# Edge lists loaded in rows of 2000 bytes, the key arithmetic on GpSimd, part of x issued later: a change to the prologue of a graph and mixture-of-experts kernel

## The chip, the cores and the metric

One core of one Trainium2 chip runs the whole program. The metric is the device time of that core in microseconds (us); lower is better. The kernel before takes 423.84 us, the median of three runs that span 423.71 to 424.52 us.

## What is computed

`x` is 1250 nodes by 512 features, with 40000 edges in two integer lists. `src` holds the node that receives and `dst` the node that is read; `dst` is sorted. The reference, cut to what matters:

```python
def gnn(x, edge_index, W1, b1, W2, b2):          # W1 512x256, W2 256x512
    h = relu(x @ W1 + b1) @ W2 + b2
    row, col = edge_index[0], edge_index[1]       # src, dst
    return h + segment_sum(h[col], row, num_segments=1250)

def ffn(x, W_gate, b_gate, W_thr, b_thr, W_exp, b_exp):   # 8 experts of 512x512
    adapted = softmax(x @ W_gate + b_gate) - sigmoid(x @ W_thr + b_thr) * 0.25
    w = adapted * (adapted >= 0);  w = w / sum(w)  (1 where the sum is 0)
    return sum over e of w[:, e] * (x @ W_exp[e] + b_exp[e])

x = x + gnn(layernorm(x), stack([src, dst]), ...)
x = x + ffn(layernorm(x), ...)
```

## The kernel before, in words

The aggregation is done as matrix products. For each window of 25 read nodes the kernel counts, on TensorE, how many edges lead from each of those nodes to each of the 1250 receiving nodes. That count matrix, moved by DMA into another layout (`a_t`), multiplies the hidden rows `r_sb`. There are 50 windows (NW), five to each of ten tiles of 125 nodes.

The counting compares keys. The receiving node is written as `src = 250*hi + lo` with hi from 0 to 4. One key is `lo`, the other is `pos = 5*dst + hi`. The 40000 edges are cut into 320 chunks (CH) of 125 consecutive edges. A column of `keys` holds a chunk, one edge on each of 125 partitions. For a window, VectorE compares the keys of its chunks with tables of positions (`places`), which gives matrices of zeros and ones in f16 (`hot`, line L552 in `compare`), and TensorE multiplies them (L788 in `count`). ScalarE takes the counts out of PSUM (L390) and SyncE's queue moves them (L282). How many chunks a window has depends on the data, so the loops of `compare` and `count` read their start and length from a table `wtab`.

All this needs a prologue, and the change is in the prologue alone. The order of each engine is written out by hand, one block of code per engine, and engines wait for one another by semaphores:

- **SyncE** (L264, L265) issues the loads of `dst_i` and `src_i`, 80 partitions (ROWS) by 4 (GJ) by 125 edges (EP), then five loads of `x_sb`, then W1 and b1.
- **GpSimd** (L311 on) fills constants: `ident`, `ones`, rows of window bounds, `c_up` and `c_down` (chunk numbers), the step table, then the five tables that ScalarE waits for (`lo_ready` 5, L342), then `zeros`, `self_pos` and `self_lo` (`self_ready` 3, L344 to L351), for which TensorE waits before its zero matmuls.
- **ScalarE** (L354 on) issues the load of partitions 112 to 124 of x (L356, semaphore `x_rest`), makes `places` for windows 0 and 1, copies the transposed keys out of PSUM into `keys` (L374, L377, semaphore `keys_placed`), and goes on with `places` for windows 2 to 4.
- **VectorE** (L448 on) reduces each chunk of `dst_i` to its least and greatest node (L455, L456), finds the chunks that meet each window (L459 to L468, semaphore `hits_ready`), computes the keys (L471 to L477, `keys_ready`), and then derives the table: L480 reads the transposed hits, L483 to L497 give three columns `wcols`, and L500 to L503 write `wtab`. It loads the table's first word, waits for `keys_placed` and begins `compare(0)`.
- **TensorE** (L709 on) waits for `hits_ready` and transposes the hits (L716), waits for `keys_ready` 1 and transposes `lo_f`, waits for 2 and transposes `pos_f` (L722), waits for `wcols_ready` 3 and turns the columns into rows (L727), waits for `self_ready` 3 and clears five banks with zero matmuls (L732), then waits for `wtab_ready` 2 and `keys_placed` 2, raises `hot_used` and starts `count(0)`.

Everything on TensorE is in this order, so a wait for keys holds back the rows of the table too. VectorE's first compare waits for `hot_used`, which TensorE raises only behind its zero matmuls:

```python
pe.wait_ge(self_ready, 3)
for k in range(5):
    z = nc.tensor.matmul(ps_g[:, k * BANK:(k + 1) * BANK], zeros[0:1, 0:128], zeros[0:1, :], ...)
z.then_inc(g_done, 1)
pe.wait_ge(wtab_ready, 2)
pe.wait_ge(keys_placed, 2)
for p in range(4):
    pe.sem_inc(hot_used[p], 1)
```

Behind the prologue come the counting and the hidden layer (to about 165 us), the second matrix product and the second layer norm (to about 210 us), and the expert loop to the end.

## Time and profile before

| | us |
|---|---|
| median of 3 runs (lowest, highest) | 423.84 (423.71, 424.52) |
| the profiled execution's own time | 425.66 |
| its span, first to last instruction | 423.8 |
| TensorE busy (share of the span) | 393.7 (93%) |
| VectorE busy | 294.4 (69%) |
| ScalarE busy | 95.8 (23%) |
| GpSimd busy | 5.1 (1%) |
| mean granted TensorE clock | 0.98 |

The profiled execution took 425.66 us, of which 423.8 us are its span and the rest lies around it. TensorE is PE in the rows (PEld its weight loads), VectorE is DVE, ScalarE ACT, GpSimd POOL, and SyncE's queue SPq. A matmul record's end is modelled, so records of one engine can overlap a little. In a timeline row the first number is the start, the second the length covered, then engine, line, operation, output and inputs, shape, and in brackets the idle time before it. A row with xN merges N records.

### The profile page before, as it was taken

Reading aid. Unit: us, or ns where it says so; the run is one execution under the profiler, and the core shown is the slowest. Engines: PE = TensorE matmul, PEld = TensorE weight load, DVE = VectorE, ACT = ScalarE, POOL = GpSimd, SP = SyncE. Lnnn points to the kernel's source line nnn. Section 1 sums busy time; section 2 is a strip of 40 time slices with the busy share of each in tenths; the row PEclk is TensorE's granted clock in tenths of the full one; section 3 lists DMA queues with packets and bytes.
Section 4 is the critical chain, followed back from the end, with each engine's and each line's share of the span. In section 5 each row is a group of like instructions: output and inputs, shape, how many; then the busy total and the mean of one; then the engine's idle time right before and its main releaser. Section 6 shows DMA issues by size and latency. Waiting matters only on the chain.

```text
span 423.8 us, 6033 instructions
## 1 busy us (share of the span) xinstructions
PE 393.7 (93%) x1964; PEld 246.0 (58%) x1964; DVE 294.4 (69%) x445; ACT 95.8 (23%) x166; POOL 5.1 (1%) x27
## 2 busy tenths in 40 slices
PE   0945999999998999979899999999999999999996
PEld 0422676666654555636566666666666666666663
DVE  3799997954656885299739767575665756657654
ACT  4621243443356551033330100101010010100000
POOL 4000000000000000000000000000000000000000
PEclk9988899999999999899899999999999999999999
DMA  8500013214133222063000203020030300000133
GB/s 179 142 13 12 25 38 108 43 34 139 37 116 111 66 68 71 0 168 127 2 0 2 99 0 101 0 95 5 0 99 0 99 0 0 0 0 0 50 97 97
DMA packets 16680, 23.75 MB, mean 56 GB/s; under 512 B 2792, under 2 KB 9555, under 8 KB 16532
## 3 DMA queue, kind: packets, MB, share of 16 engines
q1 hardware_dynamic: 16254, 22.93, 18.5%
q10 hardware_dynamic: 403, 0.53, 0.6%
q8 instruction: 12, 0.20, 0.2%
q14 instruction: 11, 0.09, 0.1%
HBM read 14.65 MB, written 2.56 MB: 41 GB/s over the span
## 4 chain that ended last, share of the span: by engine, by line
PE 81%; DVE 10%; issue 3%; DMA 2%; DVEq 2%; ACT 0%; ACTq 0%
PE ps_g L860 16%; PE ps_g L862 16%; PE ps_g L861 16%; PE ps_g L766 10%; PE ps_w L788 8%; PE ps_a L754 5%; DVE split L552 3%; DVE x_sb L595 2%; PE ps_a L755 1%; DVE stats L511 1%; DMA dst_i<-in_dst_dram 1%; PE ps_a L745 1%; PE ps_w L781 1%; PE ps_w L793 1%; DVE x_sb L603 1%
## 5 line engine op out<-in xcount | busy, mean ns | idle before, releaser
L861 PE MATMUL ps_g<-we_lo,split 128*125 128x512 f16 x320 | 122.0, 381 | 0.0
L862 PE MATMUL ps_g<-we_hi,split 128*125 128x512 f16 x320 | 122.0, 381 | 0.0
L860 PE MATMUL ps_g<-we_hi,split 128*125 128x512 f16 x320 | 122.0, 381 | 0.0
L552 DVE TENSOR_TENSOR split<-places,keys 125x1536 f16<-125x1536 int16 (+2 forms) x125 | 94.2, 816 | 7.2 <-PE ps_w L788 4.1
L671 DVE SCALAR_TENSOR_TENSOR x_sb<-ps_g,weight_s,x_sb 125x512 f32<-125x512 f32 x80 | 59.9, 749 | 56.3 <-PE ps_g L862 56.2
L788 PE MATMUL ps_w<-split 125*128 125x250 f16 x416 | 60.9, 289 | 11.6 <-DVE split L552 11.6
L676 DVE SCALAR_TENSOR_TENSOR x_sb<-late,weight,x_sb 125x512 f32<-125x512 f32 x80 | 59.9, 750 | 9.5 <-DVE x_sb L671 5.3
L788 PEld LDWEIGHTS ps_w<-split 125*128 125x128 f16 x416 | 40.0, 102 | 34.3 <-DVE split L552 21.5
L860 PEld LDWEIGHTS ps_g<-we_hi,split 128*125 128x125 f16 x320 | 43.9, 137 | 25.9 <-issue 0.6
L862 PEld LDWEIGHTS ps_g<-we_hi,split 128*125 128x125 f16 x320 | 43.9, 137 | 25.6 <-issue 0.4
L861 PEld LDWEIGHTS ps_g<-we_lo,split 128*125 128x125 f16 x320 | 43.9, 137 | 25.5 <-issue 0.6
L766 PE MATMUL ps_g<-late,r_sb 125*128 125x512 f32 (+3 forms) x120 | 54.3, 557 | 0.2
L427 ACT ACTIVATE we_hi<-stage 128x2048 f16<-128x2048 f32 x6 | 11.5, 1911 | 139.4 <-PE ps_g L862 139.4
L365 ACT ACTIVATE places<-iota_pos,win_base 125x512 int16<-125x512 int16 x50 | 35.6, 713 | 0.0
L390 ACT ACTIVATE counts<-ps_w 128x250 f32<-128x250 f32 x50 | 19.0, 380 | 72.0 <-PE ps_w L793 72.0
L568 DVE TENSOR_TENSOR late<-late 125x1250 f32<-125x1250 f32 x8 | 11.7, 1460 | 26.2 <-DMA late<-counts 26.2
L766 PEld LDWEIGHTS ps_g<-late,r_sb 125*128 125x128 f32 x120 | 19.7, 192 | 10.2 <-issue 9.3
L754 PE MATMUL ps_a<-w_sb,xn_t 128*125 128x256 f32 x80 | 19.9, 392 | 0.0
L584 DVE SCALAR_TENSOR_TENSOR we_lo<-stage,we_hi 128x2048 f16<-128x2048 f32 x8 | 18.3, 2285 | 0.0
L754 PEld LDWEIGHTS ps_a<-w_sb,xn_t 128*125 128x125 f32 x80 | 14.2, 187 | 1.8
L781 PE MATMUL ps_w<-self_lo,self_pos 128*128 128x250 f16 x50 | 13.8, 275 | 0.0
L828 PE MATMUL ps_w<-w_sb,early 128*125 128x512 f32 x24 | 11.2, 597 | 0.5 <-ACT early L412 0.5
(125 smaller groups left out, 201.1 us busy)
## 6 DMA issues: line engine op xcount, KB each, us to landing
stage<-in_L_ffn_W_exp_dram SPq DMA_DIRECT2D x8, 1024.0 KB, 5.2
late<-counts SPq DMA_DIRECT2D x50, 122.1 KB
x_sb<-in_x_dram SPq DMA_DIRECT2D x5, 448.0 KB, 9.6
out_dram<-x_sb SPq DMA_DIRECT2D x10, 224.0 KB
late<-in_L_ffn_b_exp_dram SPq DMA_DIRECT2D x1, 2000.0 KB
w_sb<-in_L_gnn_W_dram SPq DMA_DIRECT2D x2, 512.0 KB, 8.5
x_sb<-in_x_dram ACTq DMA_DIRECT2D x1, 260.0 KB
out_dram<-x_sb ACTq DMA_DIRECT2D x10, 26.0 KB
```

What stands on the lines that cost most here:

```text
L365: nc.scalar.activation(places[w % WPT][:, :, 0:SEG], iota_pos[:, :, :], ACT.Identity, bias=win_base[:, w:w + 1], scale=1.0).then_inc(pos_r ...
L390: nc.scalar.activation(counts[q][:, :], ps_w[w % 2][:, 0:LO], ACT.Copy).then_inc(win_out, 1)
L552: nc.vector.tensor_tensor(hot[hot_at(w, p)][:, 0:n, :].rearrange("p c (k x j) -> p (c k) x j", k=SEGS, j=2), places[w % WPT][:, 0:n, :].re ...
L584: nc.vector.scalar_tensor_tensor(out=we_lo[par][:, :], in0=stage[par][:, :], scalar=WSCALE, in1=we_hi[par][:, :], op0=ALU.mult, op1=ALU.su ...
L671: nc.vector.scalar_tensor_tensor(out=x_sb[:, i, :], in0=ps_exp[(TILES * par + i) % RING], scalar=weight_s[:, ds(e, 1), i], in1=x_sb[:, i, ...
L676: nc.vector.scalar_tensor_tensor(out=x_sb[:, i, :], in0=be_sb[:, ds(e, 1), :], scalar=weight[:, i, ds(e, 1)], in1=x_sb[:, i, :], op0=ALU.m ...
L754: nc.tensor.matmul(ps_a[0:R, 0:C], xn_t[:, k, :], w1_sb[:, k, :], start=(k == 0), stop=False)
L766: g = nc.tensor.matmul(ps_g[:, a:z], r_sb[:, i, c * 128:(c + 1) * 128], a_t[i % 3][:, a - c * SW:z - c * SW], start=False, stop=False, ski ...
L788: mm = nc.tensor.matmul(bank[:, 0:LO], hot[hot_at(w, p)][:, c, 0:SEG], hot[hot_at(w, p)][:, c, SEG:SEG + LO], start=False, stop=False, ski ...
L860: nc.tensor.matmul(bank, xhi[:, k, tokens[i]], hi_w, start=(k == 0), stop=False)
L861: nc.tensor.matmul(bank, xhi[:, k, tokens[i]], lo_w, start=False, stop=False)
L862: mm = nc.tensor.matmul(bank, xlo[:, k, tokens[i]], hi_w, start=False, stop=(k == KD - 1))
```

## The change

Five edits belong together.

1. `dst_i` and `src_i` are loaded so that a partition holds 500 consecutive edges, one row of 2000 bytes, and no longer four rows of 500 bytes. A partition's four chunks are now neighbours in number, so `c_up` and `c_down` count by fours.
2. The four key operations on VectorE are taken out. GpSimd computes the keys in seven instructions (of them six calculate and one is the copy of `src_i` to f32). They stand behind the tables for ScalarE and ahead of `zeros`, `self_pos` and `self_lo`. They wait for `src_in`, and among themselves for `hi_step`.
3. `pos` is finished first, `lo` second, and TensorE's transposes and ScalarE's two copies follow in that order.
4. A transpose writes every fourth column of its PSUM bank, and no longer 80 neighbouring ones, so that chunks stand in order in `keys`.
5. The load of the last 13 partitions of x moves on ScalarE's queue from the first place to behind `places` of windows 0 and 1.

The diff, without the renumbered waits of VectorE on `prep`:

```diff
-        hi_a, hi_f, lo_f, pos_f = (early[0:ROWS, k * EP * GJ:(k + 1) * EP * GJ].rearrange("p (j e) -> p j e", j=GJ)
-                                   for k in range(4))
+        hi_a, hi_f, lo_f, pos_f, dst_5 = (early[0:ROWS, k * EP * GJ:(k + 1) * EP * GJ].rearrange("p (j e) -> p j e", j=GJ)
+                                          for k in range(5))
+        src_f = sb("src_f", [ROWS, GJ, EP])[:, :, :]
...
-            sp.dma_start(dst_i[:, :, :], dst.rearrange("(j g e) -> g j e", j=GJ, e=EP)).then_inc(dst_in, 16)
-            sp.dma_start(src_i[:, :, :], src.rearrange("(j g e) -> g j e", j=GJ, e=EP)).then_inc(src_in, 16)
+            sp.dma_start(dst_i[:, :, :], dst.rearrange("(g j e) -> g j e", j=GJ, e=EP)).then_inc(dst_in, 16)
+            sp.dma_start(src_i[:, :, :], src.rearrange("(g j e) -> g j e", j=GJ, e=EP)).then_inc(src_in, 16)
...
-            nc.gpsimd.iota(c_up[:, :], pattern=[[ROWS, GJ]], base=1, channel_multiplier=1,
+            nc.gpsimd.iota(c_up[:, :], pattern=[[1, GJ]], base=1, channel_multiplier=GJ,
...
-            nc.gpsimd.iota(c_down[:, :], pattern=[[-ROWS, GJ]], base=CH, channel_multiplier=-1,
+            nc.gpsimd.iota(c_down[:, :], pattern=[[-1, GJ]], base=CH, channel_multiplier=-GJ,
...
+            pool.wait_ge(src_in, 16)
+            nc.gpsimd.tensor_scalar(hi_a, src_i[:, :, :], 1.0 / LO, -(LO - 1) / (2.0 * LO), ALU.mult, ALU.add).then_inc(hi_step, 1)
+            nc.gpsimd.tensor_copy(src_f, src_i[:, :, :]).then_inc(hi_step, 1)
+            nc.gpsimd.tensor_scalar(dst_5, dst_i[:, :, :], float(HI), None, ALU.mult).then_inc(hi_step, 1)
+            pool.wait_ge(hi_step, 3)
+            nc.gpsimd.tensor_scalar(hi_f, hi_a, ROUND, ROUND, ALU.add, ALU.subtract).then_inc(hi_step, 1)
+            pool.wait_ge(hi_step, 4)
+            nc.gpsimd.tensor_tensor(pos_f, dst_5, hi_f, ALU.add).then_inc(keys_ready, 1)
+            nc.gpsimd.tensor_scalar(hi_a, hi_f, -float(LO), None, ALU.mult).then_inc(hi_step, 1)
+            pool.wait_ge(hi_step, 5)
+            nc.gpsimd.tensor_tensor(lo_f, hi_a, src_f, ALU.add).then_inc(keys_ready, 1)
+
             nc.gpsimd.memset(zeros[:, :], 0.0).then_inc(self_ready, 1)
...
-            act.dma_start(x_sb[112:R, :, :], x.rearrange("(t p) d -> p t d", p=R)[112:R, :, :]).then_inc(x_rest, 16)
             act.wait_ge(lo_ready, 5)
...
+            act.dma_start(x_sb[112:R, :, :], x.rearrange("(t p) d -> p t d", p=R)[112:R, :, :]).then_inc(x_rest, 16)
             key_view = keys[:, 0:CH * REC].rearrange("p (c t) -> p c t", t=REC)
             act.wait_ge(keys_turned, 1)
-            nc.scalar.activation(key_view[:, :, 2:REC], ps_w[0][0:EP, 0:CH].unsqueeze(2).broadcast_to([EP, CH, REC - 2]),
+            nc.scalar.activation(key_view[:, :, 0:2], ps_w[1][0:EP, 0:CH].unsqueeze(2).broadcast_to([EP, CH, 2]),
                                  ACT.Copy).then_inc(keys_placed, 1)
             act.wait_ge(keys_turned, 2)
-            nc.scalar.activation(key_view[:, :, 0:2], ps_w[1][0:EP, 0:CH].unsqueeze(2).broadcast_to([EP, CH, 2]),
+            nc.scalar.activation(key_view[:, :, 2:REC], ps_w[0][0:EP, 0:CH].unsqueeze(2).broadcast_to([EP, CH, REC - 2]),
                                  ACT.Copy).then_inc(keys_placed, 1)
...
-            dve.wait_ge(src_in, 16)
-            nc.vector.tensor_scalar(hi_a, src_i[:, :, :], 1.0 / LO, -(LO - 1) / (2.0 * LO), ALU.mult, ALU.add).then_inc(prep, 1)
-            dve.wait_ge(prep, 6)
-            nc.vector.tensor_scalar(hi_f, hi_a, ROUND, ROUND, ALU.add, ALU.subtract).then_inc(prep, 1)
-            dve.wait_ge(prep, 7)
-            nc.vector.scalar_tensor_tensor(out=lo_f, in0=hi_f, scalar=-float(LO), in1=src_i[:, :, :],
-                                           op0=ALU.mult, op1=ALU.add).then_inc(keys_ready, 1)
-            nc.vector.scalar_tensor_tensor(out=pos_f, in0=dst_i[:, :, :], scalar=float(HI), in1=hi_f,
-                                           op0=ALU.mult, op1=ALU.add).then_inc(keys_ready, 1)
...
-            for a, (key, bank) in enumerate(((lo_f, ps_w[0]), (pos_f, ps_w[1]))):
+            for a, (key, bank) in enumerate(((pos_f, ps_w[1]), (lo_f, ps_w[0]))):
                 pe.wait_ge(keys_ready, a + 1)
                 for j in range(GJ):
-                    turned = nc.tensor.transpose(bank[0:EP, j * ROWS:(j + 1) * ROWS], key[:, j, :],
+                    turned = nc.tensor.transpose(bank[0:EP, 0:CH].rearrange("p (g j) -> p j g", j=GJ)[:, j, :], key[:, j, :],
                                                  ident[0:ROWS, 0:ROWS])
```

The order on GpSimd from the last table for ScalarE on, before (`early` is the buffer that holds `hi_a`, `hi_f`, `lo_f`, `pos_f` and now `dst_5`):

```order
L342 MEMSET keys 125x90
L344 MEMSET zeros 1x512
L345 MEMSET self_pos 128x132
L346 MEMSET self_lo 128x475
L349 AFFINE_SELECT self_pos<-self_pos 25x132 [waits self_base]
L351 AFFINE_SELECT self_lo<-self_lo 25x475
```

And on GpSimd now:

```order
L343 MEMSET keys 125x90
L346 TENSOR_SCALAR early<-src_i 80x500 [waits src_in]
L347 CAST src_f<-src_i 80x500
L348 TENSOR_SCALAR early<-dst_i 80x500
L350 TENSOR_SCALAR early<-early 80x500 [waits hi_step]
L352 TENSOR_TENSOR early<-early 80x500 [waits hi_step]
L353 TENSOR_SCALAR early<-early 80x500
L355 TENSOR_TENSOR early<-early,src_f 80x500 [waits hi_step]
L357 MEMSET zeros 1x512
L358 MEMSET self_pos 128x132
L359 MEMSET self_lo 128x475
L362 AFFINE_SELECT self_pos<-self_pos 25x132 [waits self_base]
```

Seven instructions stand between the tables and `zeros`; what TensorE's zero matmuls wait for comes behind them.

TensorE's prologue now, whose rows are the same as before but for line numbers and the PSUM banks of the keys (`ps_w1` holds `pos`, `ps_w0` holds `lo`):

```order
L720 MATMUL ps_g<-ident,hit_idx 50x80 [waits hits_ready,const_ready]
L720 MATMUL ps_g<-ident,hit_idx 50x80 x7
L726 MATMUL ps_w1<-ident,early 125x80 [waits keys_ready]
L726 MATMUL ps_w1<-ident,early 125x80 x3
L726 MATMUL ps_w0<-ident,early 125x80 [waits keys_ready]
L726 MATMUL ps_w0<-ident,early 125x80 x3
L731 MATMUL ps_a<-ident,wcols 1x50 [waits wcols_ready]
L731 MATMUL ps_a<-ident,wcols 1x50 x2
L736 MATMUL ps_g<-zeros 128x512 [waits self_ready]
L736 MATMUL ps_g<-zeros 128x512 x4
L785 MATMUL ps_w0<-self_lo,self_pos 128x250 [waits wtab_ready,keys_placed]
```

The waits on `keys_ready` at L726 are now for GpSimd, and they stand ahead of the table's rows at L731.

## Rows read from the trace of the kernel before

**Rows 1.** Busy time by stage: length, then each engine, PEclk, DMA share, GB/s
```profile
core 0: us, PE busy (x) PEld busy (x) DVE busy (x) ACT busy (x) POOL busy (x), PEclk, DMA share, GB/s
16.00:50.00 34.00, 23.51 (x129) 12.43 (x128) 33.23 (x53) 8.60 (x16) 0.00 (x0) 0.85 0.05 14
50.00:165.00 115.00, 113.69 (x624) 72.54 (x624) 83.57 (x115) 52.36 (x108) 0.00 (x0) 1.00 0.26 75
...
210.00:424.00 214.00, 210.20 (x979) 132.55 (x978) 137.64 (x185) 15.51 (x11) 0.00 (x0) 0.99 0.12 37
```

**Rows 2.** Timeline of the prologue, 0 to 17 us: DVE, PE, ACT and queues
```profile
0.74 0.37 SPq L264 DMA_DIRECT2D dst_i<-in_dst_dram  x1
0.74 0.65 ACTq L356 DMA_DIRECT2D x_sb<-in_x_dram  x1
...
6.40 0.67 DVE L455 TENSOR_REDUCE cmin<-dst_i 80x4 f32<-80x500 int32 x1 [2.94 <-DMA dst_i<-in_dst_dram]
6.91 0.70 ACT L365 ACTIVATE places<-iota_pos,win_base 125x512 int16<-125x512 int16 x1
...
9.11 0.35 DVE L468 TENSOR_TENSOR hit_idx<-hit,c_down 80x200 f32<-80x200 f32 x1
...
9.61 1.24 PE L716 MATMUL ps_g<-ident,hit_idx 80*50 80x80 f32 x8 [9.61 <-DVE hit_idx L468]
...
10.28 0.67 DVE L475 SCALAR_TENSOR_TENSOR early<-early,src_i 80x500 f32<-80x500 f32 x1
...
11.01 1.97 PE L722 MATMUL ps_w<-ident,early 80*125 80x80 f32 x8 [0.16 <-DVE early L475]
11.47 0.81 DVE L480 TENSOR_REDUCE wmax<-ps_g 50x2 f32<-50x640 f32 x1
12.18 1.24 ACT L374 ACTIVATE keys<-ps_w 125x1280 int16<-125x1280 f32 x1 [4.56 <-PE ps_w L722]
...
13.35 0.15 DVE L497 TENSOR_TENSOR wcols<-wcols,step_col 50x1 f32<-50x1 f32 x1
...
13.55 0.66 PE L727 MATMUL ps_a<-ident,wcols 50*1 50x50 f32 x6 [0.57 <-DVE wcols L497]
...
14.14 2.31 PE L732 MATMUL ps_g<-zeros 1*128 1x512 f16 x5
...
16.07 10.51 DVE L552 TENSOR_TENSOR split<-places,keys 125x1536 f16<-125x1536 int16 x12 [1.40 <-ACT places L365]
```

**Rows 3.** Chain that ended last, in order of time: start, us, what
```profile
0.74 5.63 DMA dst_i<-in_dst_dram
...
26.59 2.98 DVE stats L511 x5
```

**Rows 4.** DMA queue of SyncE: packets, MB, share of 16 engines; 1.5 to 2, 4.5 to 6 us
```profile
q1 hardware_dynamic: 45, 0.02, 33.8%
...
q1 hardware_dynamic: 351, 0.26, 115.3%
```

**Rows 5.** DMA issues: size and us from issue to landing
```profile
src_i<-in_src_dram SPq DMA_DIRECT2D x1, 156.2 KB, 5.9
```

**Rows 6.** DMA packets of all queues, 6 to 7.5 us, then 7 to 16 us
```profile
DMA packets 180, 0.36 MB, mean 239 GB/s; under 512 B 5, under 2 KB 5, under 8 KB 180
...
DMA packets 1450, 2.36 MB, mean 262 GB/s; under 512 B 80, under 2 KB 519, under 8 KB 1450
```

**Rows 7.** Timeline of POOL in the prologue
```profile
2.07 1.15 POOL L331 TENSOR_SCALAR_AFFINE_SELECT step_col<-step_col 50x1 f32<-50x1 f32 x4
3.49 0.56 POOL L337 IOTA iota_pos<- 125x500 int16 x1
...
4.19 0.17 POOL L342 MEMSET keys<- 125x90 int16 x1
4.30 0.52 POOL L344 MEMSET zeros<- 1x512 f16 x1
...
5.80 0.58 POOL L351 TENSOR_SCALAR_AFFINE_SELECT self_lo<-self_lo 25x475 f16<-25x475 f16 x1
```

More of the change, by code:

```diff
@@ L198, in gnn_moe @@
         lo_ready, self_base, self_ready = sem("lo_ready"), sem("self_base"), sem("self_ready")
-        keys_placed = sem("keys_placed")
+        keys_placed, hi_step = sem("keys_placed"), sem("hi_step")
         prep, keys_ready = sem("prep"), sem("keys_ready")
@@ L481, in _ @@
                                     AX_X, ALU.max).then_inc(prep, 1)
-            dve.wait_ge(prep, 8)
+            dve.wait_ge(prep, 6)
             nc.vector.tensor_scalar(wtmp[:, :], wmax[:, 1:2], 1.0, -1.0, ALU.max, ALU.mult).then_inc(prep, 1)
-            dve.wait_ge(prep, 9)
+            dve.wait_ge(prep, 7)
             nc.vector.tensor_scalar(wfirst[:, :], wtmp[:, :], float(CH), None, ALU.add).then_inc(prep, 1)
             nc.vector.tensor_scalar(wcols[:, 0:1], wtmp[:, :], float(CH), float(REC), ALU.add, ALU.mult).then_inc(wcols_ready, 1)
-            dve.wait_ge(prep, 10)
+            dve.wait_ge(prep, 8)
             nc.vector.scalar_tensor_tensor(out=wcount[:, :], in0=wmax[:, 0:1], scalar=wfirst[:, :], in1=ones[0:NW, 0:1],
                                            op0=ALU.subtract, op1=ALU.max).then_inc(prep, 1)
-            dve.wait_ge(prep, 11)
+            dve.wait_ge(prep, 9)
             dve.wait_ge(step_ready, 2)
@@ L493, in _ @@
                                            op0=ALU.add, op1=ALU.mult).then_inc(prep, 1)
-            dve.wait_ge(prep, 12)
+            dve.wait_ge(prep, 10)
             nc.vector.tensor_scalar(wcols[:, 1:2], wsteps[:, :], ROUND, ROUND, ALU.add, ALU.subtract).then_inc(wcols_ready, 1)
@@ L501, in _ @@
             nc.vector.tensor_copy(wtab[:, NW:2 * NW], ps_a[0:1, NW:2 * NW]).then_inc(wtab_ready, 1)
-            dve.wait_ge(prep, 13)
+            dve.wait_ge(prep, 11)
             nc.vector.scalar_tensor_tensor(out=wtab[:, 0:NW], in0=ps_a[0:1, 2 * NW:3 * NW], scalar=float(REC * WORD),
```

## The prediction, made blind

> **What bounds the kernel now.** I read the stages first, then the timeline and the chain of the prologue, then the DMA queues and GpSimd. By stage [rows 1], TensorE is busy 113.69 of 115 us from 50 to 165 us and 210.20 of 214 us from 210 us on; from 16 to 50 us VectorE is (33.23 of 34 us), since it makes the `hot` matrices. Before 16 us neither is near full, and nothing behind the prologue is touched by the diff. So the question is by how much the first compare moves, which starts at 16.07 us [rows 2]. All that follows hangs on it: the same instructions with the same waits, so I expect the rest to shift as a block.
>
> The chain in order of time [rows 3] starts with 5.63 us of waiting for `dst_i`. VectorE's reductions begin at 6.40, its last hits end at 9.46, TensorE transposes them until 10.85, but the reduction of the transposed hits starts only at 11.47, because the key operations stand ahead of it. The table's columns are done at 13.50, its rows start on TensorE at 13.55, the zero matmuls at 14.14, and the compare is 2.52 us behind the rows' start and 1.93 us behind the zeros' [rows 2]. The keys are in place at 12.18 + 1.24 + about 0.6 = 14.0 us and nobody waits for them.
>
> **Loads.** 80 partitions by 4 rows make 320 packets of 500 bytes for each list, and the new form makes 80 of 2000 bytes. The first small packets run shortly before 2 us, the last before 6 us [rows 4]: from 6 to 7.5 us only 5 packets under 512 bytes are left [rows 6]. `src_i` lands at 1.17 + 5.9 = 7.1 us [rows 5], some 1.1 us behind its last packet. Packets of 2 KB go at 262 GB/s [rows 6]. 0.32 MB for both lists then take 1.2 us, half of it for `dst_i`, and the load of `x_rest`, which ran between them on ScalarE's queue, is gone from there. 1.8 + 0.6 + 1.1 = 3.5 us for `dst_i`, 4.1 us for `src_i`; I add 0.3 us to each for the loads of x that now begin earlier, so 3.8 and 4.4. Ends: 3.5 (VectorE's two step operations end there anyway), and 6.37, no gain at all, if a load's time were mostly fixed. I take the value near the lower end because the small packets fill the queue for over 4 us. **VectorE's first reduction moves from 6.40 to 3.9, 2.5 us earlier.**
>
> **VectorE and TensorE up to the table.** The hits end at 9.46 - 2.5 = 6.96, their transposes at 8.35. With the four key operations gone, the reduction follows at 8.4 instead of 11.47, and the columns are done at about 10.4 instead of 13.50. Alone, this path would bring the compare to 10.45 + 2.52 = 12.97 us, a gain of 3.1 us. It isn't alone: TensorE passes the keys first.
>
> **GpSimd.** It ends the tables for ScalarE at 4.36 [rows 7], so it starts on the keys at about 4.45, when `src_i` has landed. No row shows it doing such arithmetic. The nearest: a select over 475 elements takes 0.58 us, an iota over 500 takes 0.56 us. I take 0.585 us for each of the five operations with one input. For the two with two tensor inputs the lower end is 0.585 and I take the double, 1.17, each input being read in its turn. The four selects on `step_col`, each waiting for the one before, take 1.15 us though they are 0.14 to 0.18 us long: a wait on itself costs about 0.15 us, and there are three. Sum: 5 x 0.585 + 2 x 1.17 + 3 x 0.15 = 5.7 us, so `lo_f` is done at 10.17 us. Two paths go on from there:
> - Transposes of `lo`: a group of four took from 10.95 to 12.18, 1.23 us [rows 2]. The rows of the table start at 11.40, later than the columns (10.4), and the compare would follow at 11.40 + 2.52 = 13.92 us.
> - The memsets and selects for `self_ready`, which took from 4.30 to 6.38, hidden until now, come behind `lo_f`: 10.17 + 2.08 = 12.25. The zero matmuls start there instead of at 14.14, and the compare at 12.25 + 1.93 = **14.18 us**. This path is the later one.
>
> GPSIMD Engine Reference of the Trainium skill, section 3.1, gives about 2.6 cycles for an element of a two-input add against one for a one-input body, at 1.2 GHz; that is an estimate of 1.08 us for 500 elements, and the sum would come out 0.2 us lower. No row here shows it.
>
> ScalarE has its `pos` copy (0.71 us, the shorter one) done before `lo` is transposed, then 1.24 us for `lo`: keys in place at 11.40 + 1.24 = 12.65 us, hidden behind the zeros. Were the zeros quick, this would be next. The load of `x_rest` is issued at 7.61 + 0.65 = 8.3 us, while ScalarE idles; even at the 9.6 us that the median load of x took it lands by 18 us, and the layer norm's statistics want it at 26.59 [rows 3] less the shift. Cost nothing; that cover is 6 us wide.
>
> **Collision of GpSimd and VectorE.** Before, GpSimd was finished at 6.38 and VectorE began at 6.40, so no row shows the two side by side. Now VectorE's five operations on hits (0.35 us each, two tensor inputs) run at 5.2 to 7.0 us beside GpSimd's first ones. Ends: nothing, and strict turns (rival 1, 2.1 us later). I take one VectorE operation, 0.4 us, since most of GpSimd's chain lies behind 7 us.
>
> **Sum.** 16.07 - 14.18 = 1.9 us less, plus 0.4 = 1.5 us less. On the profiled execution (425.66 us, of which the span is 423.8) that is 424.2; the median stands 1.8 us below that execution, so the forecast is **422.3 us**. A measurement can tell from no change about 0.2% here, 0.85 us.
>
> **Rival 1: the two engines take turns.** SBUF — State Buffer of the Trainium skill, section "Who interferes with whom", says that a VectorE instruction with two SBUF inputs contends with a GpSimd instruction that reads SBUF, and the later one is blocked for the whole instruction; the trace before can't show it. As a mechanism of this kernel: each of the five hit operations waits for a GpSimd operation in flight (0.585, once 1.17) and GpSimd for it (0.35). Alternating from 5.2 us on, the hits end at about 10.3, `lo_f` at 11.5. TensorE then ends hits at 11.7, `pos` at 12.8, `lo` at 13.8; the compare comes at 13.8 + 2.5 = 16.3 us. The loads' gain is eaten: 424.0 us, within 0.5 us of no change. For it: the overlap is sure. Against: a part of each 0.585 us is dispatch. Chance 0.25.
>
> **Rival 2, the other side: GpSimd's chain is too slow.** Everything is behind `lo_f`; before, the table's path and the zeros' had no GpSimd work in them. The compare is at `lo_f` + 2.08 + 1.93, so the gain is zero when `lo_f` is done at 12.06, when the seven operations take 7.6 us instead of 5.7. At 1.0 us for one input and 2.0 for two (1.7 times the nearest row, for f32 and integers instead of the two-byte types of those rows), they take 9.45 us, `lo_f` is done at 13.9, the compare at 17.9 us: 425.7 us. For it: I have no row of this arithmetic. Against: it is far from the nearest row, and the select and the iota, different as they are, cost almost the same for an element. Chance 0.2. It also covers that `src_i` lands no earlier than before (7.1 us): `lo_f` at 12.8, 424.6 us.
>
> **Rival 3: the spread transposes are slow.** The keys' transposes write every fourth column. PSUM — Partial Sum Buffer of the Trainium skill, "Specifications (TRN2)", says that a non-contiguous pattern slows matmuls significantly; no row here shows a strided write. If each group takes double (2.46 us), the rows start at 12.63 and the compare at 15.15: 0.9 us less than before, 422.9 us. Chance 0.1.
>
> **Numbers.** Main case 0.45. The range: at the low end GpSimd's chain takes 5.0 us with no collision (compare at 13.5, 2.6 us less, 421.2); at the high end it reaches over rival 1 and most of rival 2, to 425.2. The main case's own range is 421.2 to 423.0. Faster by over 0.2%: 0.42 from the main case, 0.05 from rival 3, 0.03 from rival 1, 0.50. Slower: 0.16 from rival 2, 0.06 from rival 1, 0.22. The rest, 0.28, is within 0.2%.
>
> **What would show it.** Right: `cmin` at 3.6 to 4.1 us; the reduction of the hits directly behind their transposes; seven GpSimd rows with `lo_f` done near 10.2; zeros starting behind `self_lo` at about 12.3; the compare at 14.2 to 14.6; the rest as before with its times shifted. Wrong: `cmin` still at 6.4; hit operations with gaps of about 0.6 us between them (rival 1); GpSimd rows of 1 us and more (rival 2); a group of four key transposes over 2 us (rival 3); or a compare that is earlier while the stretch from 16 to 50 us gives it back.

## The result, and the profile after

The changed kernel takes 427.51 us (median of 7 runs, 426.42 to 430.68); the kernel before takes 424.09 us over 7 runs (423.71 to 425.33). The ratio is 1.0073, 95% interval 1.0044 to 1.0101: slower, and outside the range that was given. A later set of twelve runs each has 427.58 against 424.67 us, 0.7% again (0.5% against all 35 runs of before in that set, whose median was 425.17). The profiled execution took 426.42 us with a span of 424.6.

The timeline of the prologue after the change (start, length, engine, line, operation; idle time before it and its releaser in brackets) answers to [rows 2, 7]:

```profile
3.39 0.66 DVE L468 TENSOR_REDUCE cmin<-dst_i 80x4 f32<-80x500 int32 x1
...
4.41 0.63 ACTq L384 DMA_DIRECT2D x_sb<-in_x_dram  x1
4.45 0.60 POOL L346 TENSOR_SCALAR early<-src_i 80x500 f32<-80x500 int32 x1
...
4.74 0.53 DVE L472 TENSOR_TENSOR above<-last_row,cmin 80x200 f32<-80x200 f32 x1
5.12 0.61 POOL L347 CAST src_f<-src_i 80x500 f32<-80x500 int32 x1
5.19 0.75 DVE L474 TENSOR_TENSOR below<-base_row,cmax 80x200 f32<-80x200 f32 x1
...
5.80 1.46 POOL L348 TENSOR_SCALAR early<-dst_i 80x500 f32<-80x500 int32 x1
...
5.98 0.65 DVE L477 TENSOR_TENSOR hit<-below,above 80x200 f32<-80x200 f32 x1
6.66 0.36 DVE L479 TENSOR_TENSOR hit_idx<-hit,c_up 80x200 f32<-80x200 f32 x1
...
7.35 1.90 POOL L350 TENSOR_SCALAR early<-early 80x500 f32<-80x500 f32 x1
...
9.33 1.23 POOL L352 TENSOR_TENSOR early<-early 80x500 f32<-80x500 f32 x1
...
9.93 0.65 DVE L492 SCALAR_TENSOR_TENSOR wcount<-wmax,wfirst,ones 50x1 f32<-50x1 f32 x1
...
10.65 1.46 POOL L353 TENSOR_SCALAR early<-early 80x500 f32<-80x500 f32 x1
...
11.47 0.15 DVE L501 TENSOR_TENSOR wcols<-wcols,step_col 50x1 f32<-50x1 f32 x1
...
12.20 1.24 POOL L355 TENSOR_TENSOR early<-early,src_f 80x500 f32<-80x500 f32 x1
...
13.49 1.13 PE L726 MATMUL ps_w<-ident,early 80*125 80x80 f32 x4 [1.74 <-POOL early L355]
...
14.54 0.65 PE L731 MATMUL ps_a<-ident,wcols 50*1 50x50 f32 x6
...
15.47 0.19 DVE L507 SCALAR_TENSOR_TENSOR wtab<-ps_a,wfirsts 1x50 int32<-1x50 f32 x1
...
15.50 2.31 PE L736 MATMUL ps_g<-zeros 1*128 1x512 f16 x5 [0.31 <-POOL self_lo L364]
...
17.06 9.65 DVE L556 TENSOR_TENSOR split<-places,keys 125x1536 f16<-125x1536 int16 x11 [1.40 <-ACT places L372]
```

`cmin` starts 3.0 us earlier than before and does not even wait. But GpSimd needs 9.0 us, from 4.45 to 13.44, for the keys: two of its five one-input operations take 0.60 and 0.61 us, the other three 1.46, 1.90 and 1.46. The columns of the table are done at 11.62 (13.50 before), and their rows start on TensorE at 14.54 (13.55 before), because the transposes of `lo` stand ahead of them and wait for GpSimd. From the rows' start to the compare it is 2.52 us, as before; the last 1.40 of them lie between the end of the last write of `wtab` (15.66) and the compare, and that stretch is 1.40 us long in all fourteen profiles of this case. The compare is at 17.06 instead of 16.07: 1.0 us later.

That is a third of the loss. The rest lies behind the prologue. The starts of ScalarE's copies of the counts (one per window) serve as marks all through the counting. The table gives the mark of the first profile before in us, and in the other columns how much later (+) the same mark is:

| window | before | before, second profile | changed | changed, second profile |
|---|---|---|---|---|
| 1 | 27.45 | -0.10 | +0.99 | +0.99 |
| 4 | 49.40 | -0.10 | +1.36 | +1.08 |
| 33 | 133.61 | -0.10 | +1.36 | +1.08 |
| 34 | 136.85 | -0.45 | +2.50 | +2.28 |
| 50 | 165.78 | -0.52 | +2.50 | +2.26 |

Between windows 1 and 4 the shift grows by 0.37 us in the first profile and by 0.09 in the second, in a stretch where the granted clock is below 1 in all four. Between windows 4 and 33 it is rigid to 0.01 us. Between 33 and 34 another 1.1 to 1.2 us is lost, and both profiles of the changed kernel agree on it. There VectorE's column sum waits for moves of counts. In the timeline the row of before is

```profile
133.61 1.46 DVE L568 TENSOR_TENSOR late<-late 125x1250 f32<-125x1250 f32 x1 [2.87 <-DMA late<-counts]
```

and of the changed kernel

```profile
136.10 1.46 DVE L572 TENSOR_TENSOR late<-late 125x1250 f32<-125x1250 f32 x1 [4.07 <-DMA late<-counts]
```

a wait of 4.07 us in place of 2.87. Behind window 50 the two profiles of the changed kernel part by the granted clock of TensorE. Windows of the first one and then of the second (length, busy times of PE, PEld, DVE, ACT, POOL, granted clock, DMA share, GB/s):

```profile
171.00:187.00 16.00, 15.53 (x65) 9.04 (x64) 8.48 (x15) 2.46 (x4) 0.00 (x0) 0.89 0.21 52
```

```profile
171.00:187.00 16.00, 15.53 (x58) 10.52 (x57) 5.81 (x10) 1.59 (x3) 0.00 (x0) 0.68 0.02 6
```

0.68 means that over half of these 16 us went at the lower of the two levels (1.2 instead of 2.4 GHz), behind a stretch from 165 us at 1.00. The last instruction starts at 421.10 us in the first and at 423.96 in the second, against 420.31 and 419.81 in the two of before. So the first profile, taken of the fastest of the seven runs, shows only 0.8 us of the 3.4.

### The profile page after: what moved, and what is told of

The parts are those of the page before. It is cut to its first block, busy times and chain, and to the rows that moved or that the text cites. A ratio compares the mean times of both kernels' runs of the same rounds, so it can differ in the third digit from the quotient of the medians.

```text
span 424.6 us, 6036 instructions
## 1 busy us (share of the span) xinstructions
PE 393.5 (93%) x1964; PEld 246.5 (58%) x1964; DVE 294.3 (69%) x441; ACT 96.1 (23%) x166; POOL 13.6 (3%) x34
## 3 DMA queue, kind: packets, MB, share of 16 engines
HBM read 14.65 MB, written 2.56 MB: 41 GB/s over the span
## 4 chain that ended last, share of the span: by engine, by line
PE 83%; DVE 8%; issue 3%; POOL 3%; DMA 1%; DVEq 1%; ACT 0%; POOLq 0%; ACTq 0%
PE ps_g L864 16%; PE ps_g L865 16%; PE ps_g L866 16%; PE ps_g L770 10%; PE ps_w L792 9%; PE ps_a L758 5%; DVE split L556 2%; PE ps_a L749 1%; PE ps_a L759 1%; DVE x_sb L599 1%; DVE stats L515 1%; DMA late<-counts 1%; PE ps_w L785 1%; PE ps_w L797 1%; DVE x_sb L607 1%
```

## The experiments

Twelve further runs were made, two of them of the two kernels unchanged. Two theories for the 9.0 us of GpSimd: A, the form of the operation decides; B, VectorE beside it does. For the rest: C, it follows from a later start or differs from run to run; D, it is a collision of transfers that the change shifted; E, it has another cause.

### The forms of GpSimd's operations, by themselves

```diff
+            one(nc.gpsimd.tensor_scalar(pc, pa, 2.0, 1.0, ALU.mult, ALU.add))
+            one(nc.gpsimd.tensor_scalar(pc, pa, 2.0, None, ALU.mult))
+            one(nc.gpsimd.tensor_scalar(pc, pa, 2.0, None, ALU.add))
+            one(nc.gpsimd.tensor_scalar(pc, pa, 2.0, 1.0, ALU.add, ALU.subtract))
...
```

> Twelve GpSimd operations over 80x500 f32 (two of them and one copy from int32), each waiting for the one before, stand at the head of its queue, where VectorE does nothing. They are extra work and delay everything, so the time says nothing. Theory A, the form decides: multiply and add takes 0.60 us, multiply alone 1.46, add and subtract 1.90, as in the changed kernel, though no engine is beside them. Theory B, VectorE beside it decides: all forms with one input take about 0.60 us here, and the add of two tensors less than 1.23.

The kernel ran once, in 445.36 us. The timeline of GpSimd in it; lines 326 to 332 are on f32 and in order multiply and add, multiply, add, add and subtract, subtract and multiply, add and add, multiply and subtract; 333 and 334 repeat the first two on int32:

```profile
2.41 0.60 POOL L326 TENSOR_SCALAR pc<-pa 80x500 f32<-80x500 f32 x1
3.10 1.46 POOL L327 TENSOR_SCALAR pc<-pa 80x500 f32<-80x500 f32 x1
4.64 1.46 POOL L328 TENSOR_SCALAR pc<-pa 80x500 f32<-80x500 f32 x1
6.18 1.88 POOL L329 TENSOR_SCALAR pc<-pa 80x500 f32<-80x500 f32 x1
8.15 1.89 POOL L330 TENSOR_SCALAR pc<-pa 80x500 f32<-80x500 f32 x1
...
12.09 1.89 POOL L332 TENSOR_SCALAR pc<-pa 80x500 f32<-80x500 f32 x1
14.07 0.60 POOL L333 TENSOR_SCALAR pc<-pi 80x500 f32<-80x500 int32 x1
14.75 1.46 POOL L334 TENSOR_SCALAR pc<-pi 80x500 f32<-80x500 int32 x1
...
16.94 0.60 POOL L336 COPY pc<-pa 80x500 f32<-80x500 f32 x1
17.62 1.23 POOL L337 TENSOR_TENSOR pc<-pa,pb 80x500 f32<-80x500 f32 x1
```

Theory A, without a remainder. With no other compute engine at work, multiply and add is the one quick form (0.60 us for 500 elements), a single operation takes 1.46, every other pair tried takes 1.88 or 1.89, and integers cost nothing extra. The gap from one operation to the next that waits for it is 0.07 to 0.09 us.

### Multiply and add everywhere

```diff
-            nc.gpsimd.tensor_scalar(dst_5, dst_i[:, :, :], float(HI), None, ALU.mult).then_inc(hi_step, 1)
+            nc.gpsimd.tensor_scalar(dst_5, dst_i[:, :, :], float(HI), 0.0, ALU.mult, ALU.add).then_inc(hi_step, 1)
-            nc.gpsimd.tensor_scalar(hi_f, hi_a, ROUND, ROUND, ALU.add, ALU.subtract).then_inc(hi_step, 1)
+            nc.gpsimd.tensor_scalar(hi_b, hi_a, 1.0, ROUND, ALU.mult, ALU.add).then_inc(hi_step, 1)
+            pool.wait_ge(hi_step, 4)
+            nc.gpsimd.tensor_scalar(hi_f, hi_b, 1.0, -ROUND, ALU.mult, ALU.add).then_inc(hi_step, 1)
...
-            nc.gpsimd.tensor_scalar(hi_a, hi_f, -float(LO), None, ALU.mult).then_inc(hi_step, 1)
+            nc.gpsimd.tensor_scalar(hi_a, hi_f, -float(LO), 0.0, ALU.mult, ALU.add).then_inc(hi_step, 1)
```

> The changed kernel with every one-input operation of the key arithmetic as multiply and add (dst_5 and the last hi_a with + 0.0, the rounding as two operations, x1 + ROUND and x1 - ROUND, through one more buffer). Theory A: all six take 0.60 us, lo_f ends at 4.45 + 6 x 0.60 + 2 x 1.23 + about 0.6 of waits = 11.1 us instead of 13.44, and the first compare moves from 17.06 to about 14.8 us; time some 421.5 to 423 us, below before. Theory B: the sum grows by one operation, lo_f at 14 us or later, compare at 17.5, time as the changed kernel or above. Theory C, that most of the loss is behind the prologue whatever the first compare does: compare at 14.8 but the time still 1 us or more above before.

425.70 us (12 runs, 423.99 to 428.50), ratio 1.0033 (1.0005 to 1.0062). Its timeline:

```profile
6.65 0.65 DVE L482 TENSOR_TENSOR hit_idx<-hit,c_up 80x200 f32<-80x200 f32 x1
...
7.17 0.60 POOL L353 TENSOR_SCALAR early<-hi_b 80x500 f32<-80x500 f32 x1
7.23 0.76 DVE L484 TENSOR_TENSOR hit_idx<-hit,c_down 80x200 f32<-80x200 f32 x1
...
9.87 1.24 POOL L358 TENSOR_TENSOR early<-early,src_f 80x500 f32<-80x500 f32 x1
...
14.74 3.56 DVE L559 TENSOR_TENSOR split<-places,keys 125x1536 f16<-125x1536 int16 x4 [1.40 <-ACT places L375]
```

`lo_f` ends at 11.1 and the compare starts at 14.74, both to 0.1 us as theory A said. And yet the kernel is slower than before, not at the 421.5 to 423 us of theory A: theory C's case. Its marks are 1.33 us ahead of before up to window 33, then 0.02 ahead at window 34 and 1.55 behind at window 36. So 2.9 us are lost, but in two ways. 1.3 us are lost by window 34, where the column sum waits. The other 1.6 us fall to the granted clock, which in this profile is 1.00 from 127 to 134 us and then, behind 2.5 us in which TensorE waited for VectorE (before 135.77), mostly at the lower of its two levels:

```profile
137.00:140.00 3.00, 3.00 (x10) 1.26 (x10) 2.71 (x6) 0.84 (x3) 0.00 (x0) 0.52 0.14 41
```

Five matmuls of `count` that take 0.70 us at 141.23 take 1.25 us at 138.52. No other profile has such a dip between windows 34 and 36.

### The keys back on VectorE

```diff
-            nc.gpsimd.tensor_scalar(hi_a, src_i[:, :, :], 1.0 / LO, -(LO - 1) / (2.0 * LO), ALU.mult, ALU.add).then_inc(hi_step, 1)
...
+            nc.vector.tensor_scalar(hi_a, src_i[:, :, :], 1.0 / LO, -(LO - 1) / (2.0 * LO), ALU.mult, ALU.add).then_inc(hi_step, 1)
...
```

> The changed kernel with the key arithmetic back on VectorE (pos before lo), the loads in rows of 2000 bytes, the spread transposes and the late load of x kept. If GpSimd's chain alone was the fault: hits end at about 6.4 us (0.36 us each again), keys at 8.6, columns at about 10.9, the first compare at 13.1 to 13.6 us, 2.5 to 3 us before the kernel before, time 421 to 421.5 us. If the spread transposes or the late load of x cost something, the compare or the layer norm's statistics behind it come later than that and the time is above 422.

421.29 us (12 runs, 420.36 to 425.47) against 424.26, ratio 0.9948 (0.9919 to 0.9976). From its timeline:

```profile
5.80 0.36 DVE L467 TENSOR_TENSOR hit_idx<-hit,c_up 80x200 f32<-80x200 f32 x1
5.88 0.73 POOL L352 TENSOR_SCALAR_AFFINE_SELECT self_lo<-self_lo 25x475 f16<-25x475 f16 x1
...
6.08 0.74 DVE L469 TENSOR_TENSOR hit_idx<-hit,c_down 80x200 f32<-80x200 f32 x1
...
8.37 1.97 PE L723 MATMUL ps_w<-ident,early 80*125 80x80 f32 x8 [0.16 <-DVE early L476]
...
13.42 4.43 DVE L553 TENSOR_TENSOR split<-places,keys 125x1536 f16<-125x1536 int16 x5 [1.40 <-ACT places L365]
```

The compare is 2.65 us earlier than before, the marks stay 2.3 to 2.7 us ahead to the end of the counting, and the time follows. The loads and the place of the `x_rest` load are a gain; moving the arithmetic is the loss. The eight key transposes take 1.97 us, to the hundredth what they took with neighbouring columns [rows 2], so writing every fourth column costs nothing.

### The place of the `x_rest` load

```diff
+            act.dma_start(x_sb[112:R, :, :], x.rearrange("(t p) d -> p t d", p=R)[112:R, :, :]).then_inc(x_rest, 16)
             act.wait_ge(lo_ready, 5)
...
-            act.dma_start(x_sb[112:R, :, :], x.rearrange("(t p) d -> p t d", p=R)[112:R, :, :]).then_inc(x_rest, 16)
```

> keys_on_dve with the load of the last 13 partitions of x back at the first place of ScalarE's queue. If the place of that load matters, it runs between the edge lists again, dst_i lands later than the 3.38 us at which VectorE could take it up there, by 0.3 to 1 us, and the compare with it; time 421.3 to 422.3 us. If the rows of 2000 bytes did it alone, nothing moves: compare at 13.4 us, time 421.3 us.

422.39 us (12 runs, 421.59 to 426.61), ratio 0.9934 (0.9893 to 0.9976) in a set whose runs of before had a median of 425.17. The median is 1.1 us above that of `keys_on_dve`, measured in another set. The timeline has

```profile
4.96 0.67 DVE L456 TENSOR_REDUCE cmin<-dst_i 80x4 f32<-80x500 int32 x1 [1.50 <-DMA dst_i<-in_dst_dram]
```

So `dst_i` lands at 4.9 instead of 6.37 us by its rows of 2000 bytes alone, and at 3.1 when `x_rest` no longer runs beside it (2.3 us behind its issue at 0.74 in `keys_on_dve`, 4.2 us here). That is more than the 0.3 to 1 us expected. The compare is at 14.64, 1.43 us before that of the kernel before and 1.22 behind that of `keys_on_dve`, and at window 50 the two profiles are 1.30 us apart. Each edit is worth about half.

### A later start alone

```diff
+            dve.wait_ge(keys_ready, 2)
+            nc.vector.tensor_scalar(scratch, hi_f, 1.0, 0.0, ALU.mult, ALU.add).then_inc(idle_step, 1)
+            nc.vector.scalar_tensor_tensor(out=scratch2, in0=hi_f, scalar=1.0, in1=src_i[:, :, :],
+                                           op0=ALU.mult, op1=ALU.add).then_inc(idle_step, 1)
```

> The kernel before with two more operations on VectorE (0.42 and 0.67 us, into buffers nobody reads) ahead of the reduction of the transposed hits, and nothing else. If all behind the first compare shifts as a block, the compare is at 17.15 us and the time 1.1 us above before (ratio 1.0026). If a later start of the counting makes what follows slower by itself (the granted clock of TensorE between 28 and 50 us), the time is 2 to 4 us above before, as for the changed kernel, and the clock of the runs is below 0.98.

424.22 us (12 runs, 423.89 to 428.69) against 424.26, ratio 1.0006 (0.9976 to 1.0037). The compare came at 16.91 (the edge list landed 0.2 us earlier this time), so 0.84 us late; the mark of window 4 is 0.42 behind, of window 34 only 0.17. Against the second profile of before (next section) the same marks are 0.52 and 0.62 us behind, and window 50 is 0.82. So the profiles don't tell whether the shift is given back, and the interval of the times holds both no loss and the 1.1 us of a block. It rules out the 2 to 4 us: a later start does not lose more by itself, which speaks against that half of theory C.

### The same two kernels again

> The kernel before, unchanged, as a second profile of it and as a measure of what two sets of runs of the same kernel differ by. Theory C1, that the wait of VectorE's column sum between 128 and 142 us is of a length that differs between executions: its marks behind 130 us lie elsewhere than in the first profile (by 0.5 us or more) though the first compare is again at 16.1 us. Theory C2, that this wait follows from the time at which the stretch begins: the marks are the same within 0.2 us.

> The changed kernel, unchanged, as a second profile and for the size of the loss. First compare at 17.1 us again. Theory C1: the marks behind 130 us move against the first profile, and the ratio to before over more runs comes down towards 1.0024, which is the 1.0 us of the first compare. Theory C2: the same marks, and a ratio of 1.006 to 1.008 again.

The kernel before has 424.67 us against 425.17 for the same kernel beside it: ratio 0.9963 (0.9928 to 0.9998), so two sets of one kernel can differ by 0.4%. The mean granted clock goes with it: it is below 0.976 in 14 of those 35 runs and in none of the twelve. The changed kernel has 427.58 us, ratio 1.0046 (1.0007 to 1.0084) to the pooled runs of before, and 1.007 to `before_again`. The marks are in the table above: at window 34 the two profiles of before lie 0.45 us apart and those of the changed kernel 0.22, while the kernels lie 2.3 to 2.9 us apart. The column sum there waits 2.87 and 1.92 us in the two of before, 4.07 and 4.06 in the two of the changed kernel. Neither theory fits in full: the wait of before differs by 1 us between executions, but the extra wait belongs to the kernel and not to the execution.

### Without a large load beside the moves

```diff
-                if w == 26:
-                    load_expert(1)
...
+            load_expert(1)
             for e in range(2, EXP):
```

> The changed kernel with the load of the second expert's weights moved from window 26 to behind the load of the expert biases (an extra edit that the kernel before doesn't have), so that no large load runs beside the moves of counts between 118 and 134 us. If those moves, held up by that load, cost the changed kernel the time beyond its first compare, the wait of the column sum near 132 us becomes about 1.5 us shorter and the time 1 to 2.5 us less than the changed kernel's, and the runs spread less. If not, the time stays within 0.5 us of it.

> The kernel before with the load of the second expert's weights moved as in after_late_expert. That edit brought the changed kernel from 427.6 to 423.7 us. If the loss behind the prologue is a collision that the change made worse, the same edit gives the kernel before clearly less, 0.3 to 1.5 us (423 to 424 us by the last runs), and the changed kernel is then about 1 us slower than it, the 1.0 us of the first compare. If the edit is worth the same 3 to 4 us in both, the collision was there before and explains nothing of the loss.

The changed kernel: 423.70 us, 3.9 us less than in the same set without this edit, more than the 1 to 2.5 us expected. The kernel before: 422.71 us against 424.03, 1.3 us less (ratio 0.9963, 0.9944 to 0.9983). The column sums, the changed kernel's first:

```profile
133.03 1.46 DVE L571 TENSOR_TENSOR late<-late 125x1250 f32<-125x1250 f32 x1 [1.69 <-DMA late<-counts]
```

```profile
131.78 1.46 DVE L567 TENSOR_TENSOR late<-late 125x1250 f32<-125x1250 f32 x1 [1.42 <-DMA late<-counts]
```

They wait 1.69 instead of 4.07 us and 1.42 instead of 2.87. With the load out of the way the changed kernel's mark is 1.3 us behind that of the kernel before at window 33, still 1.3 at window 34 and 1.0 at window 50 (first compares 17.08 and 15.67), so no extra loss is left there. The medians are 1.0 us apart, but they are of different sets, and the ratios to before in each set, 0.9962 and 0.9963, show no difference; the times alone don't settle the 1.0 us. But the marks show where the loss was: the collision of the second expert's load with the moves of counts is what the changed kernel lost between windows 33 and 34.

### What shifted the collision

The profile's DMA records hold a queue of kind "instruction", taken here for the fetch of program code: its 8 KB request below moves when VectorE's program gets longer, as the four memsets show. VectorE's program had become four instructions shorter by the change. The expert load is issued at 123.32 us before and at 124.67 after. Queue rows (packets, MB, share of 16 engines) and issue rows (KB, us from issue to landing) of before, from 124 to 125 us and from 123 to 124:

```profile
q14 instruction: 1, 0.01, 3.9%
...
stage<-in_L_ffn_W_exp_dram SPq DMA_DIRECT2D x1, 1024.0 KB, 6.6
```

and of the changed kernel from 127 to 128 and from 124 to 125.5:

```profile
q1 hardware_dynamic: 187, 0.35, 99.0%
q14 instruction: 1, 0.01, 1.9%
...
stage<-in_L_ffn_W_exp_dram SPq DMA_DIRECT2D x1, 1024.0 KB, 7.4
```

Before, the fetch comes about 1 us behind the issue, while the load's data has hardly begun; now it comes 2.8 us behind it, in the midst of the load, with the queue at 99%, and the load lands 0.8 us later. In `multadd` it is 3.2 us behind the issue and the load takes 7.5 us; in `keys_on_dve`, whose VectorE program has its old length, 0.9 us. All ten profiles that keep this load in its place agree: where the fetch comes 0.9 to 1.0 us behind the issue (seven), the load takes 6.4 to 6.7 us, where it comes 2.8 to 3.2 us behind it (three), 7.3 to 7.5. A second fetch, of 16 KB, comes 1.1 us behind the issue in two of the seven and 4.7 to 5.0 in the others, and makes no such difference. The test is to give VectorE four instructions that cost nothing:

```diff
...
+            for i in range(4):
+                nc.vector.memset(spare[:, i:i + 1], 0.0).then_inc(spare_step, 1)
             dve.wait_ge(step_base, len(STEPS))
```

> The changed kernel with four memsets of one column ahead of VectorE's first wait, where it idles, so that its program is as long again as before the change; the first compare stays at 17.06 us. Theory D, that the code fetch of 8 KB (queue 14 in the DMA records), which in the changed kernel falls into the load of the second expert's weights (2.9 us behind its issue instead of 1.0), holds up the moves of counts behind it: the fetch comes back to about 1 us behind the issue, the column sum near 133 us waits 2 to 3 us instead of 4.07, the mark of window 34 is no more than 1.2 us behind the kernel before instead of 2.5, and the time falls by 1 to 2 us to about 426. Theory E, that the extra wait has another cause (GpSimd's chain, the layout, the time of day of the load): marks and time as the changed kernel's, 427.5 us.

> multadd with the same four memsets. Its first compare was 1.33 us before that of the kernel before, and 2.9 us were lost again between windows 33 and 36. Theory D: the fetch leaves the load of the weights, the mark of window 36 is at -1.3 to -1.8 us against the kernel before instead of +1.55, and the time is 422 to 423 us instead of 425.7. Theory E: as multadd.

The changed kernel with the four memsets takes 424.75 us (12 runs, 424.45 to 428.77) instead of 427.58, ratio to before 1.0016 (0.9996 to 1.0036). `multadd` with them takes 423.03 instead of 425.70, ratio 0.9982 (0.9951 to 1.0012). The first compares did not move (17.07 and 14.74). What moved, in `multadd_pad4`: its column sum, in the timeline,

```profile
131.90 1.46 DVE L578 TENSOR_TENSOR late<-late 125x1250 f32<-125x1250 f32 x1 [1.95 <-DMA late<-counts]
```

waits 1.95 us, where in `multadd` the row is

```profile
133.59 1.46 DVE L575 TENSOR_TENSOR late<-late 125x1250 f32<-125x1250 f32 x1 [3.62 <-DMA late<-counts]
```

and its DMA rows, issue and queue from 122 to 124 us, are

```profile
q14 instruction: 1, 0.01, 1.6%
...
stage<-in_L_ffn_W_exp_dram SPq DMA_DIRECT2D x1, 1024.0 KB, 6.5
```

The fetch is back at 0.9 us behind the issue and the load at 6.5 us. In `after_pad4` the fetch is at 0.9 us too and the load at 6.7, and the column sum is

```profile
135.37 1.46 DVE L575 TENSOR_TENSOR late<-late 125x1250 f32<-125x1250 f32 x1 [2.53 <-DMA late<-counts]
```

with 2.53 us of waiting instead of 4.07. The mark of window 36 in `multadd_pad4` is 1.72 us ahead of before instead of 1.55 behind; half of that difference is the clock dip of `multadd` told of above. In `after_pad4` the step between windows 33 and 34 is 0.2 us instead of 1.1. Its mark of window 34 is 1.77 us behind before and not within the 1.2 expected, since it was already 1.57 behind at window 33.

Theory D is shown for the place: four idle instructions move the fetch, shorten the load and take 1.5 to 1.7 us off the wait of the column sum, in two kernels. The medians fall by 2.8 and 2.7 us, but across sets; against before in each one's own set the gain is 0.3% to 0.6% for the changed kernel (1.0046 or 1.0073 to 1.0016) and 0.5% for `multadd` (1.0033 to 0.9982), 1.3 to 2.4 us. How a fetch of 8 KB delays the load by 0.6 to 1.0 us and the moves behind it by 0.9 to 1.7 us is not shown; the rows don't tell the 16 DMA engines apart. Nor was it tried to move the fetch without a change in length.

### The version that beats both

> keys_on_dve with the same edit, as the version that should beat both kernels. Compare at 13.4 us, no large load beside the moves of counts: 420 to 421 us; 418 us if the edit is worth here what it was worth in the changed kernel.

422.13 us (12 runs, 419.68 to 425.22), ratio 0.9951 (0.9919 to 0.9983). It has the fastest run of all, and at window 50 its mark is 3.4 us ahead of before against 2.7 for `keys_on_dve`, but its median is above the 420 to 421 us expected and no better than that of `keys_on_dve`; the two intervals overlap almost wholly. `keys_on_dve`, at 421.29 us, is the simpler one and the version to keep: both load edits, no arithmetic on GpSimd.

The granted clock explains much of what differs between sets. The table has the median span of the runs whose mean granted clock is 0.976 or more; taken so, the kernel before gives nearly the same in three sets (422.85 in the twelve runs of `before_again`, which all count).

| kernel | such runs | median span, us |
|---|---|---|
| before, in the three sets | 24 of 29, 21 of 35, 33 of 35 | 422.35, 422.3, 422.2 |
| changed, in both sets | 4 of 7, 7 of 12 | 425.15, 425.2 |
| `after_pad4` | 11 of 12 | 422.9 |
| `multadd` | 6 of 12 | 423.5 |
| `multadd_pad4` | 9 of 12 | 420.4 |
| `after_late_expert` | 9 of 12 | 421.8 |
| `before_late_expert` | 9 of 12 | 420.8 |
| `keys_on_dve` | 10 of 12 | 419.4 |
| `dve_xrest_first` | 10 of 12 | 420.4 |
| `dve_late_expert` | 7 of 12 | 418.4 |

By these the change costs 2.9 us (2.4 against `before_again`), the four memsets give back 2.3 us in the changed kernel and 3.1 in `multadd` (part of this its clock dip), the changed kernel with the late expert load is 1.0 us slower than the kernel before with it, and the late expert load is worth 1.0 us in the version with the keys on VectorE. Five of its twelve runs had a lower clock, and its median does not show the gain.

## Why the prediction was wrong

Forecast: 422.3 us and 1.5 us faster; measured: 3.4 us slower. Two steps failed: the sum of GpSimd's chain, which turned the sign, and the block behind the prologue, which put the time out of range.

- **Loads**: the direction was right and the size too small. `cmin` was put at 3.9 and started at 3.39, free of any wait; `dst_i` landed at 3.1 us and `src_i` at 3.7 (2.4 and 2.5 us behind their issues), where 3.8 and 4.4 were taken. The 0.3 us added for the loads of x were not needed, and `x_rest` had taken 1.6 us or more of the 6.37 by itself. `x_rest` was put at 8.3 us, behind the `places` of ScalarE. In the row of L384 it is issued at 4.41 us, while the first of them runs, so the issue did not wait for them; it was still behind the edge lists.
- **GpSimd's sum, the step that decides the first compare**: 5 x 0.585 was the mis-sized term. The quick form measured 0.60 and the two-input one 1.23 (1.17 was taken), but three of the five one-input operations are of slow forms, 1.46 + 1.90 + 1.46 = 4.8 us for 1.8 us. The gaps between the seven make 0.5 us, as taken. The whole took 9.0 instead of 5.7 us. The nearest rows were a select and an iota, and nothing said that the operation pair matters. Rival 2 had the direction, with 9.45 us and a chance of 0.2; that its sum lies near the 9.0 is luck, since its 2.0 us for two inputs was too much and its 1.0 us for one input too little.
- **Which path is last**: the zeros' path was wrongly ahead. In the changed kernel the compare is 1.56 us behind the zeros' start, in the one before 1.93, so 1.93 was slack and not a length. The rows' path holds: 2.52 us before and after (17.06 - 14.54), and 2.53 in `multadd` (rows at 12.21, compare at 14.74). From `lo_f` to the compare it is 3.6 us and not 4.0, so rival 2's price was 0.4 us too high by that.
- **Collision of GpSimd and VectorE**: present, and twice the 0.4 us taken, but hidden. VectorE's five hit operations took 0.53, 0.75, 0.65, 0.36 and 0.36 us instead of 0.35 or 0.36 each, and `wcount` and `wsteps`, one column wide, 0.65 and 0.64 instead of 0.21. None of it reached the compare, since the finished columns then waited 2.9 us for TensorE. Rival 1's strict turns didn't happen: all of GpSimd's key operations took what they took alone, and `hit_idx` ran in 0.36 us inside the 1.46 us of L348. SBUF — State Buffer of the Trainium skill, "Who interferes with whom", calls the ports that the two engines share an exclusive lock; a VectorE operation of two inputs that runs unhindered inside a GpSimd operation does not fit that, and the measurement decides. It agrees that the two contend: in `keys_on_dve`, beside the select that reads SBUF, VectorE took 0.74 us for 0.36.
- **Rival 3**, slow spread transposes: wrong, 1.97 us with neighbouring columns and in `keys_on_dve` with every fourth.
- **"The rest shifts as a block", the step that put the result out of range**: true to 0.01 us from window 4 to 33, then not. The shift of the first compare alone would have given 424.8 us by the prediction's own base, inside the range. The change took four instructions from VectorE and so moved a code fetch into a 1 MB load, 110 us behind the edit. Of the 2.5 us by which window 34 is late in the first profile, 1.0 us is the prologue, 0.4 us comes between windows 1 and 4 and 1.1 us here, and the four memsets take 0.9 of this 1.1 away. The granted clock around 45 and 180 us adds scatter of some us from run to run, in every kernel: 0.89 and 0.68 from 171 to 187 us in two profiles of the changed kernel.

## What to carry to other kernels

Before work goes to GpSimd, measure the very operation forms: there the pair multiply and add costs 0.60 us where the same loop with another pair costs 1.9. Ask of each move which in-order queue then waits: here TensorE held finished columns for 2.9 us behind a transpose whose key was late. To turn the columns ahead of `lo` was not tried; `lo` is in place only at 15.89 us (14.65 + 1.24), so by these rows it could have brought the compare forward by at most some 1.2 us, an estimate. And a change in a program's length can move code fetches against large loads far behind it; marks through the whole trace, compared one by one, find such a place, and idle instructions test it.

## What the runs showed that was not expected

- GpSimd on 80x500: multiply and add 0.60 us, copy or cast 0.60, one operation 1.46, the other pairs tried 1.88 to 1.90, two tensors 1.23; int32 input costs nothing extra.
- Four instructions more or less on VectorE change where an 8 KB fetch falls in a load of 1 MB, and with it a wait by 1.5 to 1.7 us; the whole time by some 2 us of 424.
- VectorE starts its first compare 1.40 us behind the write of the table from which it takes its first word, in all fourteen profiles, whatever else had moved.
- One small load on another queue, of 130 rows of 2 KB, costs the load beside it 1.6 to 1.9 us (a landing at 4.9 us against 3.0 to 3.3).
- The same kernel measured against itself in twelve runs gave 0.9963 (0.9928 to 0.9998), so differences below 0.4% want more than that, or a comparison at like granted clock.
